# Attention of one core: pairs of long and short query tiles in turn, three shared PSUM banks and two score banks, one timetable

## The reference, cut to what matters

```python
cq = rms_norm(x @ w_qa.T, q_a_ln_w)                    # x: 1 x 2048 x 512, 384 latents
q = (cq @ w_qb.T).reshape(b, s, 16, 192)               # 128 without position, 64 with (rope)
ckv_l = rms_norm(ckv[..., :128], kv_a_ln_w)            # k_nope, v = ckv_l @ w_kvb.T
scores = einsum('bhqd,bhkd->bhqk', q_full, k_full) * scale   # causal, then softmax
out = einsum('bhqk,bhkd->bhqd', attn, v)
x = layernorm(x + out @ w_o.T)
x = layernorm(x + (x @ (weight * scale_weight[:, None]).T + bias))
```

## Time and profile before

| | us |
|---|---|
| median of 3 runs (1966.39 to 1971.29) | 1967.31 |
| the profiled execution | 1973.16 |
| its span, first to last instruction | 1971.5 |
| its attention stage, about | 163 to 1863 |
| matmuls busy in the span | 1780.0 |

### The profile page before, as it was taken

The page is one execution under the profiler, slowest core; times in us unless marked ns, Lnnn a source line. Parts: engine busy times, 40 slices in busy tenths (PEclk is TensorE's granted clock), DMA queues, the critical chain, the costliest instruction groups (busy, mean ns, idle before and its releaser), DMA issues. The chain is left out here.

```text
span 1971.5 us, 28124 instructions
## 1 busy us (share of the span) xinstructions
PE 1780.0 (90%) x8977; PEld 1425.0 (72%) x8977; DVE 1407.0 (71%) x2659; ACT 1131.7 (57%) x2247; POOL 986.8 (50%) x971
## 2 busy tenths in 40 slices
PE   5997899899999999999899899999999999998676
PEld 4566787777777787878677677877777878786432
DVE  1554667778877788877566577888888888777466
ACT  2553456566666677665345456676776766665310
POOL 2321345455655565555344455555655555555455
PEclk9998999999999999999999899999999999999889
DMA  7864111001000200010211211011002100011221
GB/s 221 314 268 160 44 43 43 33 17 58 24 28 6 81 33 27 18 42 22 75 60 49 96 49 38 17 37 50 28 6 76 38 13 32 27 39 32 92 101 54
DMA packets 53352, 122.81 MB, mean 62 GB/s; under 512 B 8736, under 2 KB 27424, under 8 KB 50848
## 3 DMA queue, kind: packets, MB, share of 16 engines
q1 hardware_dynamic: 44640, 73.41, 10.9%
q0 software_dynamic: 6848, 23.60, 3.6%
q10 hardware_dynamic: 1728, 24.12, 2.9%
HBM read 76.03 MB, written 49.28 MB: 64 GB/s over the span
## 5 line engine op out<-in xcount | busy, mean ns | idle before, releaser
L1221 POOL TENSOR_TENSOR split_p<-pool,split_p 128x512 fp32r<-128x512 f32 x544 | 702.9, 1293 | 582.5 <-ACT split_p L1158 582.3
L1027 PE MATMUL rows<-q_c,key_c 128*128 128x512 f32 x1632 | 479.1, 402 | 9.0 <-DVE q_c L1271 8.7
L1296 DVE TENSOR_TENSOR top<-rows,top 128x512 f32<-128x512 f32 x420 | 289.1, 688 | 207.2 <-ACT pool L1146 203.1
L1311 DVE TENSOR_TENSOR pool<-bank,pool 128x512 f32<-128x512 f32 x544 | 369.9, 680 | 38.2 <-PE bank L1045 38.2
L1146 ACT COPY pool<-rows 128x512 f32<-128x512 f32 x480 | 282.4, 588 | 177.8 <-PE rows L1027 176.2
L1151 ACT ACTIVATE pool<-pool 128x512 f32<-128x512 f32 x544 | 346.5, 637 | 17.5 <-DVE pool L1311 16.6
L1027 PE MATMUL rows<-q_pe,key_pe 128*128 128x512 f32 x1088 | 338.5, 392 | 0.0
L1158 ACT CAST split_p<-pool 128x512 fp32r<-128x512 f32 x544 | 333.1, 612 | 0.0
L1323 DVE TENSOR_TENSOR bank<-bank,pool 128x512 f32<-128x512 f32 x480 | 331.1, 690 | 0.1
L1027 PEld LDWEIGHTS rows<-q_c,key_c 128*128 128x128 f32 x1632 | 285.8, 190 | 51.4 <-DVE q_c L1271 11.1
L1027 PEld LDWEIGHTS rows<-q_pe,key_pe 128*128 128x128 f32 x1088 | 204.8, 188 | 45.9
(11 more groups left out here) (135 smaller groups left out, 2042.0 us busy)
## 6 DMA issues: line engine op xcount, KB each, us to landing
cq<-cq_dram SPq DMA_DIRECT2D x24, 768.0 KB, 4.8
y<-y_dram SPq DMA_DIRECT2D x64, 256.0 KB, 2.7
y_dram<-y SPq DMA_DIRECT2D x64, 256.0 KB, 2.0
wq_dram<-wq ACTq DMA_DIRECT2D x4, 2304.0 KB, 11.7
wo_dram<-wo ACTq DMA_DIRECT2D x4, 2048.0 KB, 10.2
wq<-wq_dram SPq DMA_DIRECT2D x3, 2304.0 KB, 8.7
cq_dram<-cq ACTq DMA_DIRECT2D x4, 1536.0 KB, 12.1
wo<-wo_dram SPq DMA_DIRECT2D x3, 2048.0 KB, 8.4
```

Source lines behind the costliest of these rows:

```text
L1027: mm = pe.matmul(by_head(out), k, q, start=(z == 0), stop=(z == 4))
L1221: nc.gpsimd.tensor_tensor(split_p[:, n % 3, 1, :], slot(n), stored(split_p[:, n % 3, 0, :]), ALU.subtract).then_inc(p_lo, 1)
L1296: nc.vector.tensor_tensor(out, SCORES[n % 3], slot(number(it, 0)) if t == 1 else out, ALU.max).then_inc(scores_maxed, 1)
L1311: nc.vector.tensor_tensor(slot(n), MAXES, slot(n), ALU.add).then_inc(shifted, 1)
```

## The change

The order of tiles: `PAIR_ORDER` lists the pairs of neighbouring tiles in each group, the short and the long in turn, and the odd tile of a pair comes before the even one. The first group begins with tiles 1, 0, 15, 14, 3, 2, 13, 12; the last ends with 5, 4, 11, 10, 3, 2, 1, 0. The banks: two for the scores, three for the uses. The timetable: one function gives every step a slot and a phase within it, `waits_for` names what each step needs, and `plan` gives the steps in that order, pulling forward what one needs. `spread_sum` stands in e + 2 and `y` in e + 4. The prologue comes from the same table. The tokens of a pair are loaded two pairs ahead into the half that is free, 28 loads in place of 24, and the first of them at the start of the stage. The list of tiles in `ffn_phase` follows the new order. No instruction on PE, DVE, ACT or POOL is added or taken away.

```diff
 N_ITER = G * NT
 N_TILE = G * NT * (NT + 1) // 2
+N_PAIR = N_ITER // 2
 LEAD = 7
+N_SCORES, N_AUX = 2, 3
 Y_FIRST = 10
...
+PAIR_ORDER = [[0, 7, 1, 6, 2, 5, 3, 4], [4, 3, 5, 2, 6, 1, 7, 0], [0, 7, 1, 6, 2, 5, 3, 4], [4, 7, 3, 6, 2, 5, 1, 0]]
...
+def pair_of(s):
+    return PAIR_ORDER[s // (NT // 2)][s % (NT // 2)]
...
 def tile_of(it):
-    n = it % NT
-    return n if group(it) % 2 == 0 else NT - 1 - n
+    return 2 * pair_of(it // 2) + 1 - it % 2
...
+OUT_ORDER = [tile_of(it) for it in range(N_ITER - NT, N_ITER)]
...
+def timetable():
     for it in range(N_ITER):
-        at[last_slot(it) + 1].append(("turn_max", it))
-        at[last_value(it)].append(("turn_sum", it))
-        at[last_value(it) + 1].append(("spread_sum", it))
-        at[last_value(it) + 3].append(("y", it))
-    for it in range(N_ITER - 2):
+        for t in range(keys(it)):
+            n, v = number(it, t), value_slot(it, t)
+            yield n, SCORES_AT, ("scores", it, t)
+            yield n, MAX, ("max", it, t)
+            yield v - 3, SHIFT, ("shift", it, t)
+            yield v - 2, EXP, ("exp", it, t)
+            yield v - 1, ROUND, ("hi", it, t)
+            yield v - 1, ROUND, ("sum", it, t)
+            yield v - 1, ROUND, ("lo", it, t)
+            yield v, VALUES, ("values", it, t)
+        e = last_value(it)
+        yield last_slot(it) + 1, USE_AT, ("turn_max", it)
+        yield value_slot(it, 0) - 3, SPREAD, ("spread_max", it)
+        yield e, COPIES, ("copy_sum", it)
+        yield e + 1, COPIES, ("copy_out", it)
+        yield e, USE_AT, ("turn_sum", it)
+        yield e + 2, USE_AT, ("spread_sum", it)
+        yield e + 4, USE_AT, ("y", it)
+    for it in range(-2, N_ITER - 2):
         ahead = [("q", it // 2 + 1, 2 * (it % 2) + j) for j in range(2)]
         following = [("pe", it + 3)] if it + 3 < N_ITER and not opens_group(it + 3) else []
         if opens_group(it + 2):
-            order = [("pe", it + 2), *ahead, ("turn_pe", it + 2)]
+            order = [("pe", it + 2), *ahead, ("turn_pe", it + 2), *following]
         else:
             order = [("turn_pe", it + 2), *following, *ahead]
-            following = []
         for j, use in enumerate(order):
-            at[window_slot(it, j)].append(use)
-        at[window_slot(it, 3)] += following
-    return at
+            yield (window_slot(it, min(j, 3)) if it >= 0 else it), USE_AT, use
...
+def waits_for(step):
+    what, it, *rest = step
+    if what == "scores":
+        yield ("copy_pe", it)
+        for h in range(HG):
+            yield ("q_lo", it // 2, h)
+        if number(it, *rest) >= N_SCORES:
+            yield ("max", *previous(it, *rest, N_SCORES))
+    elif what == "max":
+        yield ("scores", it, *rest)
+        if number(it, *rest) >= RING:
...
 def plan():
...
+    def give(step):
+        if step in given:
+            return
+        given.add(step)
+        for before in waits_for(step):
+            give(before)
+        if step[0] in AUX_USES:
+            if len(uses) >= N_AUX:
+                for reader in readers(uses[-N_AUX]):
+                    give(reader)
+            uses.append(step)
+        order.append(step)
+    at = {}
+    for n, phase, step in timetable():
+        at.setdefault((n, phase), []).append(step)
+        for reader in readers(step):
+            at.setdefault((n + 1, READ), []).append(reader)
+    for key in sorted(at):
+        for step in at[key]:
+            give(step)
+    return order, uses
...
+def new_tokens(s):
+    return s > 0 and pair_of(s) != pair_of(s - 1)
+CQ_COUNT = [sum(new_tokens(n) for n in range(s + 1)) for s in range(N_PAIR)]
+CQ_PLACE = [CQ_COUNT[s] % 2 for s in range(N_PAIR)]
...
-        SCORES, OUT, MAXES, TOTAL, AUX = m.bank[0:3], m.bank[3], m.bank[4], m.bank[5], m.bank[6:8]
+        SCORES, AUX = m.bank[0:N_SCORES], m.bank[N_SCORES:N_SCORES + N_AUX]
+        OUT, MAXES, TOTAL = m.bank[5:8]
...
+            def load_tokens(s):
+                at = CQ_PLACE[s] * 2 * P
+                half = pair_of(s) % 2 * 2 * P
+                sp.dma_start(stored(m.cq[:, :, :, at:at + 2 * P].rearrange("p a k n -> p (a k) n")),
+                             m.cq_dram[pair_of(s) // 2].rearrange("p (a n) -> p a n", n=512)[:, :, half:half + 2 * P]
+                             ).then_inc(cq_loaded, 16)
...
                 if s % (NT // 2) == NT // 2 - 1 and s + 1 < N_PAIR:
                     sp.dma_start(words(m.wq), m.wq_dram[group(2 * s)]).then_inc(wq_loaded, 16)
-                if s in CQ_LOADS:
-                    new = CQ_LOADS[s][0]
-                    at = new % 2 * 2 * P
...
+                new = [n for n in range(s + 1, N_PAIR) if CQ_COUNT[n] == CQ_COUNT[s] + 2]
+                if new and CQ_COUNT[s + 1] > CQ_COUNT[s]:
+                    load_tokens(new[0])
             sp.wait_ge(m.wo_free, 16 * (NCH + 1))
             sp.wait_ge(m.cq_free, 16 * (NCH + 1))
             sp.wait_ge(y_stored, 16)
             load_y(0)
+            load_tokens(1)
...
-                if USE[u] >= 2:
-                    wait_read(USES[USE[u] - 2])
+                if USE[u] >= N_AUX:
+                    wait_read(USES[USE[u] - N_AUX])
...
-                    pe.wait_ge(scores_maxed, n - 2)
-                out = SCORES[n % 3]
+                if n >= N_SCORES:
+                    pe.wait_ge(scores_maxed, n - N_SCORES + 1)
+                out = SCORES[n % N_SCORES]
...
-            return out_v[NT - 1 - u]
+            return out_v[OUT_ORDER[u]]
```

More of the change, by code:

```diff
@@ L673, in readers @@
         return [("normalise", use[1]), ("o_hi", use[1]), ("o_lo", use[1])]
-    return [("add_y", use[1])]
-def plan():
[L679 to L729, removed]
@@ L732, in needs @@
[L732 to L756, removed]
@@ L759, with previous, last_tile @@
-STEPS = list(start()) + list(plan())
-AUX_USES = ("q", "pe", "turn_pe", "y", "turn_max", "turn_sum", "spread_sum")
-USES = [u for u in STEPS if u[0] in AUX_USES]
+    if use[0] == "y":
+        return [("add_y", use[1])]
+    return []
+def previous(it, t, back):
+    n = number(it, t) - back
+    return TILES[n] if n >= 0 else None
+def last_tile(it):
+    return it, keys(it) - 1
+def waits_for(step):
[9 more added lines that the diff above has]
+        if number(it, *rest) >= RING:
+            yield ("lo", *previous(it, *rest, RING))
+            yield ("sum", *previous(it, *rest, RING))
+        if rest[0] == 1 and it >= 2:
+            yield ("turn_max", it - 2)
+    elif what == "spread_max":
+        yield ("reduce_max", it)
+        if it:
+            yield ("shift", *last_tile(it - 1))
+    elif what == "shift":
+        yield ("spread_max", it)
+    elif what == "exp":
+        yield ("shift", it, *rest)
+    elif what == "hi":
+        yield ("exp", it, *rest)
+        if number(it, *rest) >= 3:
+            yield ("values", *previous(it, *rest, 3))
+    elif what == "sum":
+        yield ("exp", it, *rest)
+        if it and rest[0] == 0:
+            yield ("copy_sum", it - 1)
+    elif what == "lo":
+        yield ("hi", it, *rest)
+    elif what == "values":
+        yield ("lo", it, *rest)
+        if it and rest[0] == 0:
+            yield ("copy_out", it - 1)
+    elif what == "copy_out":
+        yield ("values", *last_tile(it))
+        if it >= 2:
+            yield ("o_lo", it - 2)
+    elif what == "copy_sum":
+        yield ("sum", *last_tile(it))
+        if it:
+            yield ("turn_sum", it - 1)
+    elif what == "turn_max":
+        yield ("max", *last_tile(it))
+    elif what == "reduce_max":
+        yield ("turn_max", it)
+        if it >= 8:
+            yield ("spread_max", it - 8)
+    elif what == "turn_sum":
+        yield ("copy_sum", it)
+    elif what == "reduce_sum":
+        yield ("turn_sum", it)
+        if it >= 2:
+            yield ("spread_sum", it - 2)
+    elif what == "spread_sum":
+        yield ("reduce_sum", it)
+    elif what == "normalise":
+        yield ("copy_out", it)
+        yield ("spread_sum", it)
+    elif what == "o_hi":
+        yield ("normalise", it)
+        if it:
+            yield ("y", it - 1)
+    elif what == "o_lo":
+        yield ("o_hi", it)
+    elif what == "y":
+        yield ("o_lo", it)
+    elif what == "add_y":
+        yield ("y", it)
+    elif what == "q_hi":
+        yield ("q", it, *rest)
+        if it >= 2:
+            yield ("scores", *last_tile(2 * it - 3))
+    elif what == "q_lo":
+        yield ("q_hi", it, *rest)
+    elif what == "rope":
+        yield ("pe", it)
+        if it:
+            yield ("round_pe", it - 1)
+    elif what == "round_pe":
+        yield ("rope", it)
+        if it:
+            yield ("turn_pe", it - 1)
+    elif what == "turn_pe":
+        yield ("round_pe", it)
+    elif what == "copy_pe":
+        yield ("turn_pe", it)
+        if it >= 4:
+            yield ("scores", *last_tile(it - 4))
@@ new lines @@
+AUX_USES = ("q", "pe", "turn_pe", "y", "turn_max", "turn_sum", "spread_sum")
+def plan():
+    order, given, uses = [], set(), []
```

(9 more changed lines are left out.)

76 lines of the change are left out of this document (24 added, 52 removed).

## The result

The changed kernel takes 1908.39 us in the median (1907.47 to 1909.23, 4 runs) against 1967.54 of the kernel before: ratio 0.9693, 95% interval 0.968 to 0.9707, so 59 us faster. The forecast was 1912. The profiled execution took 1907.47 us with a span of 1905.8, against 1971.5 before; its mean granted clock is 0.986 against 0.978.

What follows compares the result with a forecast made beforehand. PE bounds the kernel, so gains come only from its waits and half clock. Terms -41 - 18 + 5 + 18 + 5 - 8 - 8 - 8 = -55 us gave 1912 us against the median of 1967.31; range 1872 to 1955.

Steps and rivals of the forecast that it cites:

- Spread of the sums: `spread_sum` a slot later in the attention stage: PE's 40.7 us idle before it falls to about 5; -41 us, -46 to -20.
- Three shared banks: Before `turn_pe`, `q` and `pe`: waits for readers of the use before the last go; -18 us, bounds -10 and -22.
- two score banks: `scores(n + 2)` waits for the maximum of n, late in slots behind a `pe`; +18 us, bounds +5 and +60.
- Output projection: `y` a slot later, still two behind `spread_sum`: PE arrives without its earlier stop; +5 us, bounds 0 and +20.
- Start: Start of the attention stage: third `pe` waits for tokens from DRAM, early slots pay for two banks; +5 us, +2 to +8.
- Turn of the groups: Turn of groups 1 and 2: `wq` load hidden, `wo` load issued some 2 us earlier; -8 us, bounds 0 and -16.
- Tail: Last 22 value slots: five ends of iterations instead of six, and eleven slots for chains to catch up; -8 us, 0 to -15.
- Order of the pairs: New order of tiles in the attention stage: carries the terms of the middle and the tail, 16 us by the prediction.
- Half clock: Attention stage, some 4% of it at 1.2 GHz: fewer long PE waits, so less half clock; -8 us, bounds 0 and -15.
- the waits only move on: Rival, chain from last sum to `y`: `y` waits where `spread_sum` did; +27 us, 1939 us; chance 0.15.
- Two score banks decide: Rival, scores: each maximum over 2.3 us after its scores stops PE; 2003 us if half the slots are late; chance 0.07.
- The clock falls: Rival, attention stage: all of it at the tail's clock of 0.92 instead of 0.98, 98 us more, 2010 us; chance 0.02.

## Why the prediction was right, step by step

The time is 4 us from the forecast, and each term but the tail's is there with its sign. The mechanism was right in its largest part, the spread of the sums; that the sum comes out within 4 us is in part luck: the banks brought 19 us more than said and the order 8 more, the tail brought 7 less, the later `y` cost 4 more, and the terms overlap. Their sizes, by idle time of PE and by the edits undone:

- *Spread of the sums* (-41): 40.7 to 1.5 us of idle time, 39 gone, 5 expected to stay and 1.5 did. Undone, it costs 25, also since PE then waits 6 us less before `y`. As a term by itself it was too large.
- *Three shared banks* (-18) *against two score banks* (+18): I had them cancel. Measured together they bring 19. The waits for shared banks went nearly to nothing, as said, and the scores wait 7.9 us for the maximum, below the 10 to 25 of the forecast. That wait is the one that I described: with `round_pe` behind the copy it is 0.5. But most of what `round_pe` costs is another thing. It is a price of ACT's queue, paid with three banks as well (26 us there, 20 here). ACT stops for POOL 64 times, and exponentials, roundings and copies all stand behind it in the order of the kernel.
- *Output projection* (+5): I took it on POOL's part, and that grew from 19.9 to 29.4 us, by 9.5.
- *Start* (+5): the third `pe` started at 176.49, as said at about 176, and waited 2.3 us. What I hadn't counted is that the prologue now has nothing between the second `pe` and its `turn_pe`: 3.18 us of idle time for POOL at 173.54, which is also why the waits before `turn_pe` stay above the 5.9 of the forecast.
- *Turn of the groups* (-8): 6 us. The wait for `wq` is gone (2.8 us); that for `wo` is 3.98 us in place of 7.35, as this row of PE of the changed kernel shows. SP had issued the load at 1042.00, 8.5 us ahead, and by the pages of the two profiles this load takes 8.4 in the kernel before and 8.1 here:

```profile
1050.50 4.57 PE L1148 MATMUL bank<-wo,o_t 128*128 128x512 f32 x12 [3.98 <-issue]
```

```profile
1042.00 0.43 SPq L974 DMA_DIRECT2D wo<-wo_dram  x1
```

- *Tail* (-8): nearly nothing, 18.9 to 17.5 us of idle time in the last 22 slots of `values`. This is the term that isn't there: fewer iterations end there, but those that do stop as before.
- *Order of the pairs*: I gave it the turn and the tail, 16 together. It carries 24, and by the trace of that run only some 3 us of it are idle time at the turn and 1 in the tail; the rest of the idle time lies in small waits before many operations.
- *Half clock* (-8): about right. A mean clock of 0.978 over the span is 87 us at half clock, 0.986 is 53, and half of the difference, 17 us, is an estimate of the most that this can give. The profiled execution of before is one with a lower clock than most: the others of the later sets have 0.979 to 0.983, those of the changed kernel 0.985 to 0.986, and by their middles the same estimate gives 9. The 23 us less of busy time in the stage hold this and, as an estimate, the 0.16 us for each of 34 and 35 stops, 11 us, that the first two terms count.
- Not in the sum: `turn_sum` waited 5.2 us for ACT's copy of the sums before, and waits 1.9 now.

The three edits undone singly make 25 + 24 + 19 = 68 us, and the whole change is 59. The whole also holds the prologue, the loads of the tokens and the odd tile ahead of the even one, which no run undoes, so the overlap of the three isn't known.

Of the rivals, "the waits only move on" held in the old kernel (15 of 38 us kept) and for a still later `y` (none kept), but not for the change as a whole. "Two score banks decide" would have wanted maxima late by 0.4 us in half the slots. "The clock falls" went the other way: 0.978 to 0.986. What the Trainium skill tells in "TensorE: Matmul & The Clock Gate", "A second HAM failure mode: psum-queue depth-cycling", is a kernel whose PE pauses often between groups of matmuls and whose clock swings for it. Here the pauses before the scores did grow with two banks, from 9.0 to 15.4 us, but all pauses of the stage together fell from 123.0 to 77.5, and the clock rose. With `y` one slot earlier they came to 192.8 us, and the clock was 0.955: that run agrees with the page.

The Trainium skill says in "Perfetto Trace Analysis", section "Optimization Strategy", that mixing stretches can help where the most contended engine changes over the kernel. The order of pairs mixes stretches, and it brought 24 us, but the page's condition isn't what the trace of before shows. PE is the busiest engine in both, in the window of the short tiles of the middle here (columns as in the earlier trace rows) and in that of the long tiles from 540 to 700 there:

```profile
922.00:1117.00 195.00, 169.89 (x936) 141.10 (x935) 116.60 (x222) 89.16 (x182) 80.44 (x82) 0.96 0.19 67
```

What differs is how much PE idles: 25.1 of 195 us, 13%, against 9.2 of 160, 6%.

## What to carry to other kernels

Look, on the engines that serve the bound one, for an instruction that waits for a third engine while work for the bound one is queued behind it: putting it behind that work was worth 20 to 26 us here, more than the division of the banks (13 to 19). When a wait is given a slot more, look at once at the next wait of the same chain and at what shares its buffer: the same edit was worth 15 us alone and 25 with a third shared bank and another order. A chain that is one slot short in nearly every iteration costs more than the slot (173 us, where 64 slots of 1.81 are 116), and one slot more than two brought nothing. When an edit to a timetable shows no difference, compare the two lists of steps first: one of these edits had left them the same.

## What was not expected of the hardware

Idle time of PE understates a stop. With `y` one slot earlier (one run) PE idles 119 us more before it (152.4 less 33.5), yet the kernel is 173 us slower. In the whole stage PE idles 115 us more, and the same matmuls are busy for 62 us more, 55 of them in `y`. It isn't that every `y` gets slower: the median of its matmuls is 397 to 398 ns, for 389 in the changed kernel, and the longest 767. Of the 54 `y` that the timeline shows in one piece, 28 last 4.3 to 5.5 us and the others 3.0; in the changed kernel 4 of 55 last over 4 us. The mean granted clock is 0.955 in place of 0.986.
